# Moving VectorE work inside the state-space mixer of a four-layer block: table operations, row statistics, weight rests, a one-hot

## The reference, cut to what matters

```python
# mixer, for a layernormed x: 64 heads of 64, in 8 groups that share B and C (128 wide)
proj = x @ in_proj_w.T                          # gate | x, B, C | dt
xBC  = silu(conv_bias + 4-tap causal convolution of (x, B, C))
state = state * exp(dt*A) + dt * x * B ;  y = state . C       # per token
y    = y + x * D ;  yn = group_rmsnorm(y) * norm_weight * silu(gate)
x    = x + yn @ out_proj_w.T
# feed-forward, for a layernormed x
W    = (w4 - (z4[g_idx] + 1)) * scales[g_idx]   # gate, up and down weights, 4 bits each
x    = x + (silu(x @ Wg) * (x @ Wu)) @ Wd
```

## Time and profile before

| what | value |
|---|---|
| median of 3 runs | 1378.74 us (1378.01 to 1379.72) |
| the profiled execution's own time | 1378.88 us |
| its span, first to last instruction | 1377.1 us |
| PE (TensorE matmul) busy | 1292.6 us, 94% |
| DVE (VectorE) busy | 921.6 us, 67% |
| ACT (ScalarE) busy | 677.4 us, 49% |
| POOL (GpSimd) busy | 550.4 us, 40% |
| mean granted TensorE clock | 0.975 |

### The profile page before, as it was taken

How to read it: one execution, slowest core, us unless ns; L and a number is a source line. 1 busy time by engine, 2 the same in 40 slices (tenths; PEclk the granted TensorE clock), 3 DMA queues, 4 the chain that set the end, 5 groups by cost and what they waited for, 6 DMA issues and landing times. The chain is left out here.

```text
span 1377.1 us, 20772 instructions
## 1 busy us (share of the span) xinstructions
PE 1292.6 (94%) x6262; PEld 1009.9 (73%) x6262; DVE 921.6 (67%) x1762; ACT 677.4 (49%) x1055; POOL 550.4 (40%) x557
## 2 busy tenths in 40 slices
PE   5699999999999999999999999999889999879986
PEld 4577877877887787788788778877666666667764
DVE  5876677667667666766766676677665455368995
ACT  3465565566556556656655665664523322222220
POOL 2245335444533534443453444334532334333330
PEclk9899999999999999999999999999989999999996
DMA  4211011011101101100200110010103222131200
GB/s 150 59 47 33 1 62 34 17 33 47 31 1 62 31 16 32 51 28 1 65 29 16 32 59 19 1 36 1 39 16 107 84 76 80 54 94 29 58 16 23
DMA packets 44248, 57.61 MB, mean 42 GB/s; under 512 B 10182, under 2 KB 21156, under 8 KB 43922
## 3 DMA queue, kind: packets, MB, share of 16 engines
q1 hardware_dynamic: 44178, 56.84, 13.5%
HBM read 49.87 MB, written 6.96 MB: 41 GB/s over the span
## 5 line engine op out<-in xcount | busy, mean ns | idle before, releaser
L413 POOL TENSOR_TENSOR x_w<-xs,head_g 128x512 f32<-128x512 f32 x56 | 58.6, 1047 | 280.2 <-ACT xs L522 255.5
L615 DVE SCALAR_TENSOR_TENSOR conv<-p_tile,conv_taps,conv 128x511 f32<-128x511 f32 x189 | 140.8, 745 | 27.6 <-ACT conv L489 17.3
L432 POOL TENSOR_TENSOR y<-y,x_d 128x512 f32<-128x512 f32 x56 | 72.0, 1285 | 170.7 <-DVE y L754 170.7
L726 DVE TENSOR_TENSOR em<-em,p_gb 128x512 f32<-128x512 f32 x128 | 82.2, 684 | 73.0 <-ACT em L528 73.0
L494 ACT ACTIVATE xbc<-conv 128x512 f32<-128x512 f32 x96 | 60.4, 630 | 134.2 <-DVE conv L623 77.6
L1026 PEld LDWEIGHTS p_y<-x_dt,em 128*128 128x128 f32 x896 | 108.6, 192 | 16.1 <-issue 13.0
L615 DVE SCALAR_TENSOR_TENSOR conv<-p_d,conv_taps,conv 128x511 f32<-128x511 f32 (+2 forms) x99 | 73.9, 747 | 68.9 <-ACT conv L489 65.0
L93 PE MATMUL p_tile<-xn_hi,wc_hi 128*128 128x512 f32 x252 | 110.9, 440 | 2.7 <-DVE halo L619 2.7
L93 PE MATMUL p_gate<-wr_hi,xn_hi 128*128 128x512 f32 x256 | 107.0, 418 | 1.1 <-ACT gate L510 1.1
L1026 PE MATMUL p_y<-x_dt,em 128*128 128x64 f32 x896 | 106.1, 271 | 1.0 <-DVE x_res L643 1.0
L93 PE MATMUL p_y<-wr_hi,zt_hi 128*128 128x512 f32 x256 | 103.4, 404 | 1.6 <-ACT zt_hi L498 1.6
(11 more groups left out here) (336 smaller groups left out, 3301.0 us busy)
## 6 DMA issues: line engine op xcount, KB each, us to landing
w_raw<-w SPq DMA_DIRECT2D x112, 256.0 KB, 2.8
q_words<-q SPq DMA_DIRECT2D x33, 256.0 KB, 2.6
h_ring<-h_lo_rows SPq DMA_DIRECT2D x6, 704.0 KB, 5.0
h_lo_rows<-h_rest SPq DMA_DIRECT2D x11, 256.0 KB, 2.0
x_res<-x SPq DMA_DIRECT2D x8, 256.0 KB, 4.5
out<-out_t SPq DMA_DIRECT2D x8, 256.0 KB, 2.1
h_lo_rows<-h_rest SPq DMA_DIRECT2D x11, 128.0 KB, 1.8
decay_lhs<-cum_parts SPq DMA_DIRECT2D x64, 6.0 KB
```

Of the source, the lines that this page charges most:

```text
L413: pool.tensor_tensor(by_head(x_w[:]), by_head(xs[:, c % 2, :]), heads(DTW, c), ALU.mult)\
L432: pool.tensor_tensor(y[:, c % 2, :], y[:, c % 2, :], x_d[:], ALU.add).then_inc(s_txd, 1)
L615: ve.scalar_tensor_tensor(out=conv[:, s, sh:], in0=p[:, 0:HALF - sh], scalar=conv_w[:, bass.ds(g, 1), j, tap], in1=conv[:, s, sh:], op0=AL ...
L726: ve.tensor_tensor(m, m, gm.unsqueeze(1).broadcast_to([P, HG // 2, P]), ALU.mult)\
```

## The change

The table operations of the last group are cut into six pieces: two in each of the chunks 2, 3 and 4, one ahead of the products with the decays and one ahead of the wait for the product inside the chunk. `row_stats(c - 1)` moves from ahead of L754 to behind the new state, and in chunk 7 to behind z. `row_rest` moves from ahead of L777 to behind z. In chunk 0 of every group all four output-weight rests stand behind the last taps. In chunk 7 TensorE's first spread moves ahead of the row transposes. The two `hot_down` operations leave the feed-forward layer's own list and stand ahead of the last residual. SyncE's `keep_operands` moves from chunk 4 to chunk 5.

```diff
-                if last and c == CH:
+                if last and c == CH + 1:
                     keep_operands()
-                if last and c == CH + 1:
                     tables()
...
-        def small_operands():
+        def small_operands(piece):
...
+            if piece == 0:
+                ve.wait_ge(s_q_in, 16 * 4)
...                                  # 2 operations
+            if piece == 1:
...                                  # 3 operations
+            if piece == 2:
+                ve.wait_ge(s_q_ve, 5)
...                                  # 3 operations
+            if piece == 3:
+                ve.wait_ge(s_q_ve, 8)
...                                  # 2 operations
+            if piece == 4:
+                ve.wait_ge(s_q_ve, 10)
...                                  # 1 operation
+            if piece == 5:
+                ve.wait_ge(s_q_ve, 11)
...                                  # 1 operation
                 if not first:
                     z_rest(n - 1)
+                if last and c in OPERANDS_IN:            # (2, 3, 4)
+                    small_operands(2 * (c - OPERANDS_IN[0]))
                 ve.wait_ge(s_gm, 2 * (n + 1))
...
-                    if c == 2:
-                        small_operands()
...
                     tile_taps(*tile, range(2, TAPPED[tile[3]]))
-                if last and c > 0:
-                    row_stats(c - 1)
...
                 for tile in later:
                     tile_taps(*tile, range(1))
-                if c == 0:
-                    w_rest(g, TILES + KT)
-                    w_rest(g, TILES + KT + 1)
-                for k in rows_in(last, c):
-                    row_rest(k)
+                if last and c in OPERANDS_IN:
+                    small_operands(2 * (c - OPERANDS_IN[0]) + 1)
+                if last and 0 < c < NC - 1:
+                    row_stats(c - 1)
                 if last and c == NC - 1:
                     up.dequant(ve, 0, 0, 0)
                 ve.wait_ge(s_intra, n + 1)
...
                 ve.tensor_tensor(z[:], y[:, c % 2, :], gate[:], ALU.mult).then_inc(s_z, 1)
+                for k in rows_in(last, c):
+                    row_rest(k)
+                if last and c == NC - 1:
+                    row_stats(c - 1)
                 for tile in later:
                     tile_taps(*tile, range(1, TAPPED[tile[3]]))
                 if c == 0:
-                    w_rest(g, TILES + KT + 2)
-                    w_rest(g, TILES + KT + 3)
+                    for k in range(GW // P):
+                        w_rest(g, TILES + KT + k)
...
         row_rest(NC - 2)
+        up.hot_down(ve)
         residual(LAST, NC - 1)
...
                     out_product(n - 1)
+                if last and c == NC - 1:
+                    pe.wait_ge(s_e, 2 * (n + 1))
+                    up.spread(pe, 0, 0, 0)
                 for k in rows_in(last, c):
                     row_transpose(k, n)
...
-                if last and c == NC - 1:
-                    pe.wait_ge(s_e, 2 * (n + 1))
-                    up.spread(pe, 0, 0, 0)
...
-    def vector(ve):
+    def hot_of_down(ve):
         ve.wait_ge(f_d, 32)
         ve.wait_ge(f_zero, 3)
         one_hot(ve, gi_d0, hot_d[0:PART * GD, 0:L], 1)
         one_hot(ve, gi_d1, hot_d[0:PART * GD, L:NI], 1)
 
+    def vector(ve):
```

More of the change, by code:

```diff
@@ L238, in mixer @@
     LAST = NC * G - 1
+    OPERANDS_IN = (2, 3, 4)
     VE_LO = [TILES, TILES + 1] + list(range(TILES + KT, WT))
@@ L673, in row_rest @@
                              xn_hi[:, :, k * P:(k + 1) * P].bitcast(F32), ALU.subtract).then_inc(l2_lo, 1)
-        def small_operands():
[L677 to L680, removed]
+        def small_operands(piece):
             index = ((slice(0, NGI), GU), (slice(NGI, NGI + NGD), GD))
-            for cols, groups in index:
-                ve.tensor_scalar(q_index_f[:, cols], q_index[:, cols], 0.0, float(groups), ALU.is_lt, ALU.mult)\
+            if piece == 0:
+                ve.wait_ge(s_q_in, 16 * 4)
+                ve.tensor_copy(q_parts[0], q_raw).then_inc(s_q_ve, 1)
+                ve.tensor_scalar(q_zero4, q_zero, q_shift, 15, ALU.logical_shift_right, ALU.bitwise_and)\
@@ L685, in small_operands @@
                     .then_inc(s_q_ve, 1)
[L686 to L698, removed]
+            if piece == 1:
+                for cols, groups in index:
+                    ve.tensor_scalar(q_index_f[:, cols], q_index[:, cols], 0.0, float(groups), ALU.is_lt, ALU.mult)\
+                        .then_inc(s_q_ve, 1)
+                ve.wait_ge(s_q_ve, 2)
+                ve.tensor_tensor(q_rest, q_raw, q_parts[0], ALU.subtract).then_inc(s_q_ve, 1)
@@ new lines, in small_operands @@
+            if piece == 2:
+                ve.wait_ge(s_q_ve, 5)
+                ve.tensor_scalar(q_zero1, q_zero4, 1.0, None, ALU.add).then_inc(s_q_ve, 1)
+                ve.tensor_tensor(q_index_f[:], q_index_f[:], q_index, ALU.add).then_inc(s_q_ve, 1)
+                ve.tensor_copy(q_parts[1], q_rest).then_inc(s_q_ve, 1)
+            if piece == 3:
+                ve.wait_ge(s_q_ve, 8)
+                for cols, groups in index:
+                    ve.tensor_scalar(q_index_f[:, cols], q_index_f[:, cols], 0.0, float(groups - 1), ALU.max, ALU.min)\
+                        .then_inc(s_q_ve, 1)
@@ L700, in group @@
+            if piece == 4:
+                ve.wait_ge(s_q_ve, 10)
+                ve.tensor_tensor(q_rest, q_rest, q_parts[1], ALU.subtract).then_inc(s_q_ve, 1)
+            if piece == 5:
+                ve.wait_ge(s_q_ve, 11)
+                ve.tensor_copy(q_parts[2], q_rest).then_inc(s_q_ve, 1)
         def group(g, last):
@@ L1383, in swiglu_up @@
     up.tables, up.zeros, up.rest, up.round_w, up.dequant, up.hot_gu = tables, zeros, rest, round_w, dequant, hot_of_gu
-    up.spread, up.spread_down, up.product = spread, spread_down, product
+    up.hot_down, up.spread, up.spread_down, up.product = hot_of_down, spread, spread_down, product
     return sync, gpsimd, scalar, vector, tensor
```

## The result

| kernel | median us | all runs | ratio to before |
|---|---|---|---|
| before | 1379.23 | 1378.01 to 1380.74 (4) | |
| after | 1370.72 | 1369.91 to 1371.40 (4) | 0.9933 [0.9921, 0.9945] |

The change takes 8.5 us off; 1368.8 was forecast, in a range of 1363.8 to 1373.0. The profiled execution after took 1370.79 us with a span of 1369.0, against 1378.88 and 1377.1 before. In the code after, the lines stand 2 to 11 numbers further on: the decay product is L995 (was L985), z L791 (L786), its transposes L922 (L912), the row transposes L953 (L943), the rests L655 (L653).

A forecast was written before the change was run, and what follows sets the result against it. TensorE, busy 700.95 of 712.00 us in groups 1 to 6, bounds the kernel, so only its waits cost time. Terms sum to -8.15, with the clock -10.0, from 1378.88 to 1368.9; median forecast 1368.8, range 1363.8 to 1373.

The forecast's parts named there:

- the rests: Groups 0 to 6: rests behind the taps remove TensorE's wait in chunk 1, 1.3 us per group, -9.1 us in all.
- z's hold: Last group, chunks 1 to 4: z stands still while GpSimd's earlier-started state_dec runs, ending at +2.19 instead of +1.43 us.
- the one-hot: Seam: with hot_down earlier, spread_down needs no wait and the next product starts at 1036.14 instead of 1038.0, -1.9 us.
- the clock behind the one-hot: Behind the seam: without the gap the product runs at full clock, 1.9 us gained, bounds 0 and 3.6.
- signs for right: L985 wait under 0.2 us, chunk 1's output product unwaiting, stretch 7.8 us shorter, spread_down gapless, z 1.2+ us, row_transpose(6) waiting 2+.
- first sign for wrong: In the trace, a new TensorE wait for a VectorE rest (L653) would show the forecast wrong.
- rival D: Chunk 0's fourth rest falls behind GpSimd's x_w and x_dt: +1 instead of -9.1, about 1382.5 us; chance 0.04.
- Chunks 0 to 4: Last group: chunks 0 and 1 together +0.4, chunk 2 -1.05, chunk 3 +0.45, chunk 4 +1.3 us.
- Chunk 7 and the seam: row_rest(5), statistics, power and GpSimd's L1211 ahead of row_norm(6) delay row_transpose(6) from 1022.98 to near 1024.9, +1.9 us.
- A: Last group gains too, pieces and z not held up: 2.7 us there and 1.7 of clock, 1364.4 us; chance 0.2.
- B: Seam stays at 1.2 GHz: low clock carried one product further, later product not saved, 1372.6 us; chance 0.17.
- C: Nothing of the rests' move arrives because TensorE meets an equal wait in chunk 1: 1377.9 us; chance 0.04.

The follow-up runs named there:

- rests_only: The kernel before with only the four output-weight rests moved behind the taps of chunk 0; 1372.74 us, ratio 0.9947 to before.
- xw_waits: The kernel after with GpSimd's x_w and x_dt of chunk 1 held back until the fourth rest is done; 1367.06 us, 0.9906 to before.
- pool_order: The kernel after with GpSimd's power in the last group moved behind the next chunk's state_dec; 1365.46 us, 0.9898 to before.
- best: After plus xw_waits, pool_order, pieces_early, statistics behind the state only in chunks 2 and 3, row_rest ahead of y, seam as before, hot_down kept; 1364.94 us.
- best_spread: The kernel best with TensorE's first spread behind the carried-state product again; 1362.47 us, 0.9875 to before.
- hot_only: The kernel before with only hot_down moved ahead of the last residual; 1376.74 us over ten runs, 0.9981 to before.
- pieces_early: The kernel after with each chunk's second table piece beside the first, ahead of the products with the decays; 1367.26 us, 0.9917 to before.
- rests_back: The kernel after with the first two output-weight rests back ahead of y; 1378.36 us, 0.9989 to before.
- seam_back: The kernel after with chunk 7's statistics and row_rest(5) at their places of before; 1365.81 us, 0.99 to before.

## Why the prediction was right, and which terms were off

The mechanism of the largest term, the rests, held, and so did those of z's hold and of the one-hot; 1368.8 was 1.9 us below the median. That it came so near is in part luck: chunk 5's +1.3 and the start's +1.4 stood in no term, nor did the 2.28 us that chunk 7's output product gave, and the clock behind the one-hot came out near its term for a reason that no run shows.

**The signs.** Of the signs for right, three came as written: L985's wait (L995 now) for the taps is gone from every middle group, z takes 1.53 us or more in chunks 1 to 4, and spread_down follows row_transpose(7) without a gap. Two came in part: the output product of chunk 1 waits 0.18 us for the last rest, which is at once the first sign for wrong, and the six middle groups are 5.3 us shorter instead of some 7.8. One did not come: row_transpose(6) waits 0.56 us, not over 2; the gap, 2.98 us, stands ahead of the second spread, which waits for row_rest(5). And behind the seam's fourth product TensorE ran at 1.2 GHz (p_y, 0.63), which was a sign for wrong, too.

**The rests: -9.1 forecast, -6.3 measured.** The wait for the taps went entirely. The step that failed is the one that all four rests "still end at 561.85". This stretch lies 2.27 us earlier after (551.09 against 553.36 for the product ahead of y), so by the forecast the fourth rest was due at 559.58; it ended at 560.47. The 0.6 us "to spare" cover most of these 0.89: the output product, forecast at 562.5 - 2.27 = 560.24, started at 560.52. That and a tenth lost further on make a middle group -0.9 instead of -1.3. It is rival D's mechanism in small, and D's counter-argument, that x_w's copy comes "when the fourth rest has begun", is what failed with it: x_w started at 558.78, 0.15 us ahead of the fourth. rests_only has the same slow rests without the other edits, and xw_waits has the full 1.3 back. The Trainium skill, "SBUF — State Buffer", "Who interferes with whom", counts a VectorE instruction with two SBUF inputs among those that contend with a GpSimd instruction that reads SBUF. The rests agree: 944 ns in the mean, one of four held for 0.8 us, and 747 ns with x_w held back.

**Chunks 0 to 4.** That z takes over 1.2 us was forecast from one row (1.24) and an order that hung on 0.15 us; all four z came so, and with the order turned round (pool_order) z has its 0.69. In chunk 1 TensorE was to be 0.4 late when it enters chunk 2's products: it is, 0.92 early at the z_transpose and then 1.31 of wait for the taps. At the head of chunk 3 it stands at -0.87 against chunk 0 (forecast -0.65), of chunk 4 at -0.74 (-0.2), of chunk 5 at +0.31 (+1.1). So chunks 2, 3 and 4 cost -1.3, +0.1 and +1.05 where -1.05, +0.45 and +1.3 stood: every sign right, each some 0.3 too dear. One reason can be read in chunk 2: y stands 3.28 us behind L760 (943.12 - 939.84) where 3.7 were forecast. The sum let the three table operations start when y + x_d ended; the held pair ended 0.09 us behind it, so its own time was in the hold already.

**Chunk 5: 0 forecast, +1.3 measured.** The forecast looked at VectorE alone. TensorE had idled 2.37 us for z at 974.15, and the stretch behind it ran at a mean clock of 0.66, the gate product's first matmuls at 0.63 us instead of 0.39. That is the whole of the 1.3: the gate product starts 1.97 us behind z_transpose in both kernels, so the 0.30 that L995 waits for the row_rests stay covered as forecast, and it ends 1.4 later. The longer wait needn't be the reason. Behind 1.34 us, as before, rests_only lost 0.7 in the same stretch, and behind 1.13 us in both, chunk 5 took 15.29 in best and 14.56 in best_spread.

**Chunk 7 and the seam: +1.9 forecast, +1.7 measured.** From chunk 7's z_transpose to row_transpose(6) stand 16.49 against 17.07 us, but 2.28 of that is chunk 7's output product (2.98 to the next instruction instead of 5.26, granted 1.00 instead of 0.50). That product's speed was no term of the sum; with it at the slower rate the seam would be at +1.7. The wait of 1.61 us for zt_hi ahead of it is the same before and after, so the wait alone does not decide; why it ran at 1.2 GHz before and at 2.4 after is open.

**The one-hot: -1.9 forecast, -2.1 measured; the clock behind it: -1.9 forecast, -1.7 measured.** The first product is at 2.99 us and full clock. The one behind it, p_y, still fell (4.58 us at 0.63), where before both did. The forecast took the missing gap as the reason for the clock. That isn't shown: in rests_only the gap of 2.39 us is there and 1.8 us of the clock's price are gone as well, only from the other product.

**The start.** Group 0 begins 1.4 us later in the profile after, and in the other kernels between 0.9 and 2.8 us later, in hot_only alone 0.1, whatever they move; the change touches nothing there. The forecast had no term for it. Summed: -6.3 + 0.9 - 2.1 - 1.7 + 1.4 = -7.8, of 8.1.

**The rivals.** A (the last group gains as well) was wrong as a forecast of this kernel, but its price was fair: with pool_order and pieces_early the last group does gain, and in best its chunks take 4.6 us less than in after, about the 4.5 that A's full bounds give for chunks 1 to 4. B (the seam stays at 1.2 GHz) did not come at its price: the last output product is slow before and after (4.92 and 4.63 us), and of the two products past the one-hot one is still slow. C (nothing of the rests arrives) is excluded by rests_only. D is in the 2.8 us missing from the rests.

The 0.9 us of rests_back are thus a balance: the one-hot alone brings 2.4 by hot_only's median, and the last group and the rest of the seam take 1.5 of it back.

## What to carry to other kernels

Work moved into an idle slot of VectorE is priced by what GpSimd does in that slot: look up both engines' rows there, with the copy that releases GpSimd, before you count the move as free. When a small operation delays the release of a long GpSimd one by a tenth of a microsecond, the order of the two engines' instructions can turn; ask which of two nearly simultaneous instructions comes first, and if it matters, fix the order by a wait or by the program's order. And before you put a change of TensorE's speed down to an edit, look for an execution in which the edit is missing and the speed changed all the same: here rests_only was one, and the part of the kernel that no edit touched differed by up to 3.5 us.

## What the runs showed of the hardware that was not expected

Very small VectorE operations are held by a GpSimd operation as a large one is: two TENSOR_SCALARs on 128x8 took 0.94 us together beside y + x_d (0.24 without it), a CAST of 128x128 took 1.08 beside x_dt (0.22). An operation with one input in PSUM was not: zt_lo at 933.06 took 0.69 beside x_w. A held operation ends soon behind the one that held it: z and the fourth rest 0.55 us behind state_dec and x_w, the small ones 0.09 behind y + x_d and x_dt.

The stretches at 1.2 GHz don't follow from the last wait alone. Chunk 7's output product stood behind the same 1.61 us wait in the kernels before, after, rests_only, pool_order and pieces_early, and took 5.26, 2.98, 4.28, 4.51 and 4.51 us; one kernel, best, ran in 1359.31 to 1365.51 us, and its fastest run had a mean granted clock of 0.982 where the others had 0.976 or 0.977. Edits whose own rows show 0.5 to 3.0 us (seam_back, pieces_early, pool_order) moved the medians by 3.5 to 5.3. In the profiled executions of pool_order and pieces_early 2 us of this are clock behind chunk 7's z_transpose; for seam_back's median no run separates it.
